# Regrouping sixteen batch tiles into chunks of 2, 3, 4, 4 and 3, and moving one exponential behind a copy

## The chip, the cores and the metric

The kernel runs on one NeuronCore of a Trainium2 chip. The core has TensorE (PE in the profile), VectorE (DVE), ScalarE (ACT), GpSimd (POOL) and SyncE (SP), each with its own in-order program, and DMA queues that SP, ACT and POOL feed. The metric is the device time of one execution in microseconds; lower is better.

## The reference, cut to what matters

A recommendation model scores 2048 items (B). A history of 50 item embeddings per item is weighted by a softmax attention; the five features are gated, paired, sent through two cross layers of 1920 x 1920, and through a small head.

```python
target = item_table[item_id] + gelu(ln(item_emb @ mm_w + mm_b))
seq_emb = item_table[item_seq]                       # B x 50 x 128, gathered
x = concat([t, seq_emb, t - seq_emb, t * seq_emb])
scores = (relu(x @ aw1 + ab1) @ aw2 + ab2)[..., 0]   # masked where item_seq == 0
hist_feat = einsum('bs,bsd->bd', softmax(scores), seq_emb)
sparse = stack([like, view, item_id_feat, item_img_feat, hist_feat])
w = sigmoid(relu(mean(sparse) @ se_w1 + se_b1) @ se_w2 + se_b2)   # the gate
se = sparse * w
dnn_in = concat([se, pairwise products of se @ bil_W and se])     # B x 1920
xc = dnn_in
for i in range(2):
    xc = dnn_in * (xc @ cross_K[i] + cross_bias[i]) + xc          # 1920 x 1920 each
h = gelu(ln(xc @ w1 + b1)); h = gelu(ln(h @ w2 + b2))
out = sigmoid(h @ w3 + b3)
```

## The kernel before

The batch is 16 tiles of 128 items. A program in two kinds of parts works on them.

**The opening.** Attention, gate and pairing of the first `TILES[0]` tiles (4 before) run alone, in steps of `opening_step` on each engine. Their features stay in SBUF as X0h and X0l (a high and a low part, both fp32r). The first pass of the cross layers can't start before them.

**The chunks.** Each of the `CHUNKS` chunks (4 before, of 4 tiles each) then makes one pass over all cross weights: 30 steps (2 layers of 15 output features), each of 3 units. A unit is one weight block of 128 x 640 (320 KB), which SP fetches (L402), ACT copies to Wh (`w_hi`, L808), DVE subtracts to Wl (`w_lo`, L1148), and PE uses in 15 matmuls (`products`, L550 to L552), each of T x 128 moving columns, where T is the chunk's number of tiles. So a pass has 1350 such matmuls whatever T is, 128x128 weights each. After them `w1_products` (L581 to L583) multiplies the result by w1: 15 x T x 3 matmuls of 512 columns, while the next chunk's features come back from DRAM (`rows_load`, L814) and are split (`r_hi`, `r_lo`). The first dense layer's output of a chunk goes through the rest of the head (`fc_...` helpers) in the first ten steps of the next chunk; after the last chunk it stands alone as a tail.

**What else a step carries.** While chunk c runs, the attention of the tiles of chunk c + 1 is woven into its steps by `make_plan`. A tile has five groups of ten history rows. GROUP_STEPS says in which steps a group's transposes stand: for 4 tiles at 1 + 6j + g, for 3 tiles at 1 + 8j + g + g // 3. A group takes three steps: `grp` (transposes on PE, `copy_eT` on ACT, `times_target` on DVE), `open` (PE `hidden`, DVE `hidden_max`, L1053, PE `score`, L503) and `summed` (DVE `softmax_max`, which ends with L1067; ACT `exps` and `weigh`, L759 to L767; DVE `history`, L1087). A tile ends with `fold` (DVE), `gate` (ACT's exponential of five numbers, L772, then DVE `tail_gate_apply`, L1113), `lift` and `pair`. In steps with history, DVE waits for `weigh` before its sum.

**Gathers.** POOL issues the 800 gathers of history rows (L415) in order of tiles. The buffer `e` holds one tile's five groups, so the rows of group g of tile t are gathered once `history` has freed group g of tile t - 1 (`e_free`, L437). From tile AHEAD = TILES[0] + 1 on, POOL also waits for the landing after every five gathers (L443).

**Order.** Every engine's order is written out by hand in `step(p)`; between engines there are only semaphores. Weights are converted three units ahead (LOOK), six raw blocks are in flight (WRING). The last tile of the opening (LAST = TILES[0] - 1) splits its fifth group in two (TAPER).

The ACT part of a step before is this (L909 to L922):

```python
unit(c, 3 * k)
...
if p.n or p.layer:
    x_hi(*((c, p.layer, p.n - 1) if p.n else (c, 0, FEATS - 1)))
if p.gate is not None:
    tail_gate()
if p.grp:
    copy_eT(0)
unit(c, 3 * k + 1)
```

Of the kernel before, what the change touches and what calls it, by code (L numbers as in the profile page):

```python
# [15 lines left out]
HID = 64  # L16
FIELDS = 5
FEATS = FIELDS + FIELDS * (FIELDS - 1) // 2
TILES = (4, 4, 4, 4)
CHUNKS = len(TILES)  # L20
BASE = tuple(sum(TILES[:c]) for c in range(CHUNKS))
TPC = max(TILES)
NB = TPC * P
# [6 lines left out]
TAPER = EVEN[:NG - 1] + (((NG - 1) * GRP, 3), ((NG - 1) * GRP + 6, 2))  # L30
LAST = TILES[0] - 1
AHEAD = TILES[0] + 1

# [50 lines left out]
class Step:  # L84


    def __init__(self, chunk, k):
# [4 lines left out]
        self.fold = self.gate = self.lift = self.pair = None  # L92
        self.fc = TILES[chunk - 1] if chunk else 0

# [46 lines left out]
def build(nc, idx_d, table_d, cate_d, embT_d, rows_d, cols_d, mmw_d, aw1_d, bil_d, kx_d, w1_d, w2_d, out_d, ntiles):  # L141
    assert sum(TILES) == ntiles
    with ExitStack() as ctx:
# [96 lines left out]
        def pairs(T):  # L240
            return [range(2 * q, min(2 * q + 2, T)) for q in range((T + 1) // 2)]
# [127 lines left out]
        def fresh(c, layer, n):  # L369
            return (x1f, x0f)[layer][:, 0:TILES[c], n, :]  # L370
# [341 lines left out]
        def _(act):  # L712
            af = nc.scalar.activation

            def done(ins):
                link(act, act_done, ins)
# [11 lines left out]
            def head_fetch(t):  # L728
                b = t % SBUFS
                act.dma_start(S[:, b, 3, :], img_d[t]).then_inc(img_landed[b], DMA)  # L730


            def copy_eT(u, n=SUB):
                act.wait_ge(tp_ready, 1).then_inc(tp_ready, -1)
                act.wait_ge(eT_free, 1).then_inc(eT_free, -1)  # L735
                done(af(eT[:, u, 0:n * P], tps[:, 0:n * P], ACT.Copy))  # L736
                act.sem_inc(tp_free, 1)
                act.sem_inc(eT_ready, 1)
# [10 lines left out]
            def copy_tT(t):  # L749
                act.wait_ge(tp_ready, 1).then_inc(tp_ready, -1)  # L750
                done(af(tT[:, t % 2, :], gps, ACT.Copy))
                act.sem_inc(tp_free, 1)
                act.sem_inc(tT_ready, 1)

            def exps(t, g):
                first, n = groups(t)[g]
                act.wait_ge(sc_ready, 1).then_inc(sc_ready, -1)
                if g:
                    af(corr[:, g:g + 1], nmax[:, g - 1:g], ACT.Exp, scale=-1.0, bias=nmax[:, g:g + 1])  # L759
                done(af(pw[:, g % 2, 0:2 * n], sc[:, first:first + 2 * n], ACT.Exp, bias=nmax[:, g:g + 1], accum_out=gsum[:, g:g + 1]))  # L760
                act.sem_inc(p_ready, 1)

            def weigh(t, g):
                first, n = groups(t)[g]
                for s in range(2 * n):
                    x = e[:, first + s, :]
                    last = af(x, x, ACT.Copy, scale=pw[:, g % 2, s:s + 1])  # L767
                last.then_inc(weighed, 1)

            def tail_gate():  # L770
                act.wait_ge(gate_ready, 1).then_inc(gate_ready, -1)
                af(g5[:], g5[:], ACT.Exp, scale=-1.0).then_inc(gexp_ready, 1)  # L772

            def tail_copy(t, opened=False):
                if 0 < t <= TILES[0]:
                    act.wait_ge(dn_free, 1).then_inc(dn_free, -1)
                elif t:
                    act.wait_ge(dnn_stored, DMA * (t - TILES[0]))
                if opened:
                    act.wait_ge(tp2_ready, 1).then_inc(tp2_ready, -1)  # L780
                    done(af(dn[:, 0:FIELDS, :].rearrange("p s b -> p (s b)"), tps2, ACT.Copy))
                    act.sem_inc(tp2_free, 1)
                else:
                    act.wait_ge(tp_ready, 1).then_inc(tp_ready, -1)
                    done(af(dn[:, 0:FIELDS, :].rearrange("p s b -> p (s b)"), tps, ACT.Copy))
                    act.sem_inc(tp_free, 1)
                act.sem_inc(S_free, 1)
                act.sem_inc(seT_ready, 1)

            def tail_store(t):  # L790
                act.wait_ge(dn_full, 1).then_inc(dn_full, -1)
                act.dma_start(dnn_d[t], dn[:, 0:FEATS, :]).then_inc(dnn_stored, DMA)
# [24 lines left out]
            def r_hi(c, k):  # L817
                for i, (a, _) in enumerate(LOADS):
                    if k == a:
                        act.wait_ge(rows_landed[i], c * DMA)  # L820
                act.wait_ge(x0_free, 1).then_inc(x0_free, -1)
                T = TILES[c]
                af(X0h[:, 0:T, k, :], x1f[:, 0:T, k, :], ACT.Copy).then_inc(hi_done, 1)

            def x_hi(c, layer, n):
                act.wait_ge(xnew_ready, 1).then_inc(xnew_ready, -1)
                Xh = X1h if layer == 0 else X0h
                af(Xh[:, 0:TILES[c], n, :], fresh(c, layer, n), ACT.Copy).then_inc(xhi_done, 1)
# [6 lines left out]
            def fc_gelu1(j, bank=FCB):  # L835
                act.wait_ge(fT_ready, 1).then_inc(fT_ready, -1)
                for k in range(H1 // P):
                    last = af(h1_T(j)[:, k, :], xps[:, bank, k * P:(k + 1) * P], ACT.Gelu, scale=col("g1", k), bias=col("lb1", k))
                done(last)
                if bank == FCB:  # L840
                    act.sem_inc(bank4_free, 1)
                act.sem_inc(g_ready, 1)

            def fc_gelu2(js, bank=FCB):
                act.wait_ge(fT_ready, 1).then_inc(fT_ready, -1)
                n = len(js)
                for k in range(H2 // P):
                    last = af(g2T(js, k), xps[:, bank, n * k * P:n * (k + 1) * P].rearrange("p (t b) -> p t b", t=n),
                              ACT.Gelu, scale=col("g2", k), bias=col("lb2", k))
                done(last)  # L850
                if bank == FCB:
                    act.sem_inc(bank4_free, 1)
                act.sem_inc(g_ready, 1)

            def fc_exp(c):
                T = TILES[c]
                act.wait_ge(logits_ready, 1).then_inc(logits_ready, -1)
                if c:
                    act.wait_ge(out_stored, c * DMA)
                done(af(probs[0:T, :], mps[0:T, 0:P], ACT.Exp, scale=-1.0, bias=neg_b3[0:T, :]))  # L860
                act.sem_inc(bank4_free, 1)
                act.sem_inc(lexp_ready, 1)

            def fc_out(c):
                act.wait_ge(probs_ready, 1).then_inc(probs_ready, -1)
                act.dma_start(out_d[BASE[c]:BASE[c] + TILES[c], :], probs[0:TILES[c], :]).then_inc(out_stored, DMA)
# [5 lines left out]
            def unit(c, b):  # L872

                if c * STREAM + b + LOOK < TOTAL:
                    w_hi(c * STREAM + b + LOOK)
# [22 lines left out]
            def step(p):  # L898
                c, k, T = p.chunk, p.k, p.fc

                if c and k == 0:
                    r_hi(c, FEATS - 1)
                if T and k == T + 6:
                    fc_exp(c - 1)
                if T and k == T + 7:
                    fc_out(c - 1)
                if p.pair is not None:
                    tail_copy(p.pair)
                unit(c, 3 * k)  # L909
                if p.fetch is not None:  # L910
                    head_fetch(p.fetch)
                if p.summed:
                    exps(*p.summed)
                    weigh(*p.summed)
                if p.n or p.layer:
                    x_hi(*((c, p.layer, p.n - 1) if p.n else (c, 0, FEATS - 1)))
                if p.gate is not None:
                    tail_gate()

                if p.grp:  # L920
                    copy_eT(0)
                unit(c, 3 * k + 1)  # L922
                if T and 2 <= k < T + 2:
                    fc_gelu1(k - 2)

                if p.grp:
                    copy_eT(1)
                elif p.swing is not None:
                    copy_tT(p.swing)
                if T and k == T + 3:  # L930
                    fc_gelu2(pairs(T)[0])
                if T > 2 and k == T + 4:
                    fc_gelu2(pairs(T)[1])
                unit(c, 3 * k + 2)
                if p.pair is not None:
                    tail_store(p.pair)
                if T and k in (1, T + 2):
                    fc_sd(T)
# [23 lines left out]
            for c in range(CHUNKS):  # L962
                for p in chunks[c]:
                    step(p)
                w1_stage(c)
# [478 lines left out]
```

## Time and profile before

| what | value |
|---|---|
| time, median of 2 runs | 2119.64 us (2118.11 to 2121.18) |
| span of the profiled execution | 2115.6 us |
| PE busy | 1937.3 us, 92% |
| DVE busy | 1337.0 us, 63% |
| ACT busy | 904.3 us, 43% |
| POOL busy | 894.1 us, 42% |
| DMA | 220.31 MB, mean 104 GB/s |

How to read it: a record's duration of a matmul is modelled and overlaps the next one's, so a rate is read from the distance between two starts. "Idle before" in brackets is how long the engine had nothing to do ahead of the row, and what released it (DVEq, ACTq, POOLq, PEq: the engine's own sequencer at a semaphore wait of that line). PEclk is the clock that TensorE was granted, 1.00 being 2.4 GHz and 0.50 being 1.2 GHz. Rows of a window give, after the window's length, each engine's busy microseconds.

### The profile page before, as it was taken

To read this page: it belongs to the slowest core of one execution; us is meant where nothing else is said; L and a number is where in the kernel's file an instruction comes from. 1 tells how busy PE (TensorE), PEld (TensorE's weight loads), DVE (VectorE), ACT (ScalarE), POOL (GpSimd) and SP (SyncE) were. 2 spreads that over 40 slices of the span, in tenths; PEclk is the share of its full clock that TensorE was granted. 3 is DMA by queue.
4 is the path that set the end of the run, shared out by engine and by line. 5 is a ranking of instruction groups with operands and counts; after the bars stand their busy time and mean duration, and the time that the engine had idled before them with its cause. 6 is when DMAs were issued, how large, how long until landed. Compare 5 with 4: busy or idle time off the path is not lost. (4 is left out here: it accounts for less than half of the span.)

```text
span 2115.6 us, 32889 instructions
## 1 busy us (share of the span) xinstructions
PE 1937.3 (92%) x9608; PEld 1518.8 (72%) x9608; DVE 1337.0 (63%) x2242; ACT 904.3 (43%) x1969; POOL 894.1 (42%) x854
## 2 busy tenths in 40 slices
PE   1765659999999999999999999999999999999997
PEld 1444437777777887777777886777777888888885
DVE  4564564767777755667777755666777664445543
ACT  1443443444444335654445235654445243322223
POOL 7777776555655512555555601555560000000000
PEclk7666568999999999999999999999999999999998
DMA  5111123334434452334434452334432442333330
GB/s 164 50 51 50 49 51 102 104 102 129 120 109 122 143 190 68 100 95 127 118 111 123 148 175 63 100 111 115 120 107 90 129 158 81 89 99 96 97 91 15
DMA packets 99679, 220.31 MB, mean 104 GB/s; under 512 B 21792, under 2 KB 27184, under 8 KB 99376
## 3 DMA queue, kind: packets, MB, share of 16 engines
q1 hardware_dynamic: 63072, 136.90, 21.5%
q0 software_dynamic: 27136, 55.63, 10.4%
q10 hardware_dynamic: 9296, 25.70, 3.2%
q8 instruction: 80, 1.31, 0.3%
q14 instruction: 95, 0.78, 0.1%
HBM read 205.29 MB, written 12.85 MB: 103 GB/s over the span
## 5 line engine op out<-in xcount | busy, mean ns | idle before, releaser
L415 POOL DMA_INDIRECT e<-in_item_table,idx_all x800 | 842.9, 1054 | 651.9 <-issue 303.8
L1148 DVE TENSOR_TENSOR Wl<-raw,Wh 128x640 fp32r<-128x640 f32 (+1 forms) x420 | 338.2, 805 | 286.6 <-DVEq L1147 283.0
L808 ACT ACTIVATE Wh<-raw 128x640 fp32r<-128x640 f32 (+1 forms) x420 | 301.8, 722 | 494.7 <-ACTq L807 493.7
L550 PE MATMUL xps<-X0h,Wh 128*128 128x512 f32 x900 | 364.7, 405 | 0.0
L550 PE MATMUL xps<-X1h,Wh 128*128 128x512 f32 x900 | 359.4, 399 | 0.0
L552 PE MATMUL xps<-X0h,Wl 128*128 128x512 f32 x900 | 352.1, 391 | 0.0
L551 PE MATMUL xps<-X0l,Wh 128*128 128x512 f32 x900 | 351.7, 391 | 0.0
L552 PE MATMUL xps<-X1h,Wl 128*128 128x512 f32 x900 | 351.0, 390 | 0.0
L551 PE MATMUL xps<-X1l,Wh 128*128 128x512 f32 x900 | 350.7, 390 | 0.0
L767 ACT ACTIVATE e<-e,pw 128x128 f32<-128x128 f32 x800 | 242.8, 388 | 15.4 <-ACTq L138 15.4
L552 PEld LDWEIGHTS xps<-X0h,Wl 128*128 128x128 f32 x900 | 169.4, 188 | 37.2
L552 PEld LDWEIGHTS xps<-X1h,Wl 128*128 128x128 f32 x900 | 168.9, 188 | 36.5
L550 PEld LDWEIGHTS xps<-X0h,Wh 128*128 128x128 f32 x900 | 169.8, 189 | 34.1 <-issue 2.1
L550 PEld LDWEIGHTS xps<-X1h,Wh 128*128 128x128 f32 x900 | 169.2, 188 | 33.6 <-issue 1.0
L551 PEld LDWEIGHTS xps<-X0l,Wh 128*128 128x128 f32 x900 | 170.1, 189 | 31.2
L551 PEld LDWEIGHTS xps<-X1l,Wh 128*128 128x128 f32 x900 | 169.4, 188 | 32.2
L1087 DVE TENSOR_REDUCE hist<-e 128x128 f32<-128x1280 f32 (+1 forms) x65 | 156.0, 2399 | 49.3 <-DVEq L1085 49.3
L736 ACT ACTIVATE eT<-aps 128x640 f32<-128x640 f32 x141 | 98.1, 696 | 166.6 <-ACTq L735 166.1
L1039 DVE TENSOR_TENSOR teT<-eT,tT 128x1280 f32<-128x1280 f32 x79 | 117.7, 1490 | 64.3 <-DVEq L1037 64.3
L492 PE MATMUL hps<-eT,A 128*64 128x512 f32 (+2 forms) x640 | 137.4, 509 | 19.7 <-PEq L486 19.6
L467 PE MATMUL aps<-ident,e 128*128 128x128 f32 x700 | 109.7, 290 | 37.9 <-issue 27.5
L496 PE MATMUL hps<-teT,A 128*64 128x512 f32 (+2 forms) x640 | 134.4, 499 | 0.0
(149 smaller groups left out, 2181.4 us busy)
## 6 DMA issues: line engine op xcount, KB each, us to landing
raw<-in_cross_K SPq DMA_DIRECT2D x360, 320.0 KB
raw<-in_w SPq DMA_DIRECT2D x60, 256.0 KB
e<-in_item_table,idx_all POOLq DMA_INDIRECT x800, 2.5
dnn_scratch<-dn ACTq DMA_DIRECT2D x12, 960.0 KB, 4.2
x1f<-dnn_scratch ACTq DMA_DIRECT2D x3, 2048.0 KB, 9.3
x1f<-dnn_scratch ACTq DMA_DIRECT2D x3, 1792.0 KB, 15.0
dn<-in_embT SPq DMA_DIRECT2D x1, 1024.0 KB, 5.3
img_scratch<-dn ACTq DMA_DIRECT2D x1, 1024.0 KB, 4.6
```

The source lines that it names most:

```text
L415: nc.gpsimd.indirect_dma_start(out=dst, out_offset=None, in_=table, in_offset=bass.IndirectOffsetOnAxis(ap=idx_all[:, t, s:s + 1], axis=0) ...
L467: last = nc.tensor.transpose(tps[:, s * P:(s + 1) * P], e_sub(t, g, u, s), ident[:])
L492: last = mm(hsum[u * HID:(u + 1) * HID, a:b], A12[:], eT[:, u, a:b], start=True, stop=False)
L496: last = mm(hsum[u * HID:(u + 1) * HID, a:b], A3[:], teT[:, u, a:b], start=False, stop=True)
L550: m0 = mm(out, wh, Xh[:, 0:T, k, :], start=(k == 0), stop=False)
L551: m1 = mm(out, wh, Xl[:, 0:T, k, :], start=False, stop=False)
L552: m2 = mm(out, wl, Xh[:, 0:T, k, :], start=False, stop=(k == FEATS - 1))
L767: last = af(x, x, ACT.Copy, scale=pw[:, g % 2, s:s + 1])
L808: af(Wh[:, split_slot(w), 0:n], raw[:, rs, 0:n], ACT.Copy).then_inc(hi_done, 1)
L1039: v.tensor_tensor(teT[:].rearrange("p u (s b) -> p (u s) b", b=P), eT[:].rearrange("p u (s b) -> p (u s) b", b=P), tT[:, par:par + 1, :].t ...
L1087: done(v.tensor_reduce(hist[:] if g else acc[:, par, :], x, AX.X, ALU.add))
L1148: v.tensor_tensor(Wl[:, rs, 0:n], raw[:, rs, 0:n], Wh[:, slot, 0:n].bitcast(F32), ALU.subtract).then_inc(lo_done, 1)
```

## The change

`TILES` becomes five chunks of 2, 3, 4, 4 and 3 tiles. The opening then prepares two tiles, and five passes over the cross weights are made instead of four. LAST becomes 1 and AHEAD 3; the largest chunk is still 4 tiles, so no buffer changes its size. And in ACT's step, the gate's exponential is issued after the first copy of transposes.

```diff
-TILES = (4, 4, 4, 4)
+TILES = (2, 3, 4, 4, 3)
...
                 if p.n or p.layer:
                     x_hi(*((c, p.layer, p.n - 1) if p.n else (c, 0, FEATS - 1)))
+                if p.grp:
+                    copy_eT(0)
                 if p.gate is not None:
                     tail_gate()
-
-                if p.grp:
-                    copy_eT(0)
                 unit(c, 3 * k + 1)
```

## Rows read from the trace of the kernel before

**Rows 1.** The profile's first part: busy time and its share of the span.
```profile
PE 1937.3 (92%) x9608; PEld 1518.8 (72%) x9608; DVE 1337.0 (63%) x2242; ACT 904.3 (43%) x1969; POOL 894.1 (42%) x854
```

**Rows 2.** Windows: opening, four chunks, tail. Columns: length, PE, PEld, DVE, ACT, POOL, PEclk, DMA.
```profile
0.00:324.40 324.40, 177.34 (x824) 121.24 (x825) 173.12 (x354) 118.90 (x325) 248.75 (x246) 0.65 0.25 69
324.40:778.40 454.00, 453.65 (x2325) 356.98 (x2325) 316.31 (x512) 202.61 (x458) 256.53 (x241) 1.00 0.43 126
778.40:1250.30 471.90, 463.91 (x2395) 365.15 (x2394) 328.63 (x545) 230.09 (x496) 223.98 (x212) 1.00 0.40 119
1250.30:1724.30 474.00, 465.36 (x2395) 365.73 (x2394) 326.72 (x538) 230.21 (x496) 164.88 (x156) 1.00 0.37 110
1724.30:2083.30 359.00, 359.00 (x1603) 296.50 (x1601) 180.92 (x268) 107.54 (x163) 0.00 (x0) 1.00 0.31 90
2083.30:2115.60 32.30, 18.04 (x74) 13.23 (x72) 11.31 (x29) 14.96 (x31) 0.00 (x0) 0.76 0.00 1
```

**Rows 3.** Timeline of PE, last chunk: first and last of 52 matmuls of 512 columns.
```profile
2000.09 0.39 PE L551 MATMUL xps<-X1l,Wh 128*128 128x512 f32 x1
...
2011.65 0.39 PE L551 MATMUL xps<-X1l,Wh 128*128 128x512 f32 x1
```

**Rows 4.** Timeline of DVE: the gates of the first and third opening tile.
```profile
122.79 0.83 DVE L1113 TENSOR_TENSOR S<-S,tiny 128x640 f32<-128x640 f32 x1
...
263.10 0.83 DVE L1113 TENSOR_TENSOR S<-S,tiny 128x640 f32<-128x640 f32 x1
```

**Rows 5.** Timeline of PE: scores (matmuls of two columns) ending two neighbouring steps.
```profile
623.53 1.17 PE L503 MATMUL hps<-cols,hidT 128*128 128x2 f32 x10
...
638.51 1.17 PE L503 MATMUL hps<-cols,hidT 128*128 128x2 f32 x10
```

**Rows 6.** Timeline of PEld: the weight loads of one of these scores.
```profile
623.31 1.31 PEld L503 LDWEIGHTS hps<-cols,hidT 128*128 128x128 f32 x10
```

**Rows 7.** Timeline of DVE, first chunk, layer 0: from one group's `softmax_max` to the next's.
```profile
396.51 0.21 DVE L1067 TENSOR_SCALAR nmax<-tiny,nmax 128x1 f32<-128x1 f32 x1
...
399.98 0.82 DVE L1053 TENSOR_TENSOR hidT<-hps,negT 128x640 f32<-128x640 f32 x1 [1.83 <-DVEq L1052]
400.72 0.21 DVE L1074 SCALAR_TENSOR_TENSOR rsum<-rsum,corr,gsum 128x1 f32<-128x1 f32 x1
401.19 2.46 DVE L1087 TENSOR_REDUCE hist<-e 128x128 f32<-128x1280 f32 x1 [0.26 <-DVEq L1085]
...
410.21 0.21 DVE L1067 TENSOR_SCALAR nmax<-tiny,nmax 128x1 f32<-128x1 f32 x1
```

**Rows 8.** Timeline of ACT: the weighing that belongs to the first of these.
```profile
397.61 3.04 ACT L767 ACTIVATE e<-e,pw 128x128 f32<-128x128 f32 x10 [0.18 <-ACTq L138]
```

**Rows 9.** Groups by line and shape (mean ns after the comma): DVE at 512 and 256 columns.
```profile
L1165 DVE TENSOR_TENSOR x0f<-X0h,X0l 128x512 f32<-128x512 f32 x60 | 41.7, 695 | 14.3 <-DVEq L1153 10.7 <-DVEq L138 2.9
...
L1218 DVE TENSOR_TENSOR dn<-xps,rows 128x256 f32<-128x256 f32 x16 | 6.7, 417 | 9.6 <-DVEq L1217 9.6
```

**Rows 10.** Timeline of DVE: the first chunk's first history sum, after which e is freed.
```profile
371.16 2.47 DVE L1087 TENSOR_REDUCE acc<-e 128x128 f32<-128x1280 f32 x1 [0.26 <-DVEq L1085]
```

**Rows 11.** Timeline of POOL: the first gather that this frees, and the 150th history row from it on.
```profile
374.61 1.01 POOL L415 DMA_INDIRECT e<-in_item_table,idx_all  x1 [11.49 <-POOLq L437]
...
658.48 0.95 POOL L415 DMA_INDIRECT e<-in_item_table,idx_all  x1 [0.30 <-issue]
```

**Rows 12.** DMA issues: size of one, median us to landing (`rows_load`, its larger part).
```profile
x1f<-dnn_scratch ACTq DMA_DIRECT2D x3, 2048.0 KB, 9.3
```

**Rows 13.** The line of the gate's exponential: its records, and ACT's waits ahead of it.
```profile
L772 ACT ACTIVATE tiny<-tiny x16: 189/194/211, 121.8 to 1649.5; 128x5 f32<-128x5 f32 x16
...
  ACTq L771: 22.1, 4
```

**Rows 14.** Timeline of PE: a wait inside the third chunk.
```profile
1315.54 0.88 PE L604 MATMUL xps<-ident,dn 128*128 128x128 f32 x3 [3.50 <-PEq L602]
```

**Rows 15.** Window around it, columns as in the windows above.
```profile
1300.00:1330.00 30.00, 26.50 (x133) 20.48 (x131) 18.54 (x31) 16.79 (x33) 14.43 (x14) 0.94 0.29 82
```

## Prediction

> **What bounds the kernel now.** I read the page's busy shares first, then a table of windows by stage, then timelines. PE is busy 92% of the span [rows 1]. By stage it is the bound in all four chunks (full in the first and the last, 98% in the others) and not in the opening: there 324.4 us pass with PE at half of its time and at a granted clock of 0.65, while POOL is busy 77% of it with gathers [rows 2]. A chunk's PE time comes out of one number: 52 matmuls of 512 columns start within 11.56 us, so one per 226.7 ns [rows 3]. A pass has 1350 of them and w1_products 180, so 1530 x 0.2267 = 346.9 us. The first chunk took 454.0 [rows 2], so the attention of four tiles costs PE 107.1, or 26.8 a tile. The two middle chunks took 18 to 20 more than the first, the head of the chunk before. The last, with the head and no tiles, took 359.0, so 12.1 for the head alone.
>
> **The opening.** It gets two tiles shorter. The gates of the first and third tile are 140.3 us apart [rows 4], that is 70.2 a tile, paced by 50 gathers; the last tile's taper keeps its distance to the first product. New opening: 324.4 - 140.3 = 184.1 us. Saved: 140.3.
>
> **What a pass costs now.** The work of the two tiles doesn't vanish: chunks must weave 14 tiles instead of 12, 2 x 26.8 = 54 us of PE. The columns that PE streams stay the same, 16 tiles' worth, but there are 1350 matmuls more, and what each costs beyond its columns is 226.7 - 512/2.4 = 13.4 ns. If that is a fixed cost, one of 256 columns takes 120 ns and one of 384 takes 173.4, and the fifth pass adds 18 us; if it scales with the columns, 113 and 170. 128x128 weight loads alone, beside matmuls of two columns, come (1.31 - 0.19)/9 = 124 ns apart [rows 6], and their matmuls (1.17 - 0.25)/9 = 102 ns [rows 5]. So a load is barely covered by 256 columns; I take 120 and keep 113 and 125 as ends. By PE alone the new chunks would be: first, 162 + 20 (w1) + 80 (3 tiles) = 263 us; second, 234 + 31 + 107 + 9 (head of two tiles) = 381; and the sum of all would be 2047. A rule of the Trainium skill ("TensorE: Matmul & The Clock Gate", Back-to-back issue gap) gives columns/2.4 + 2.5 ns, so 109 for 256 and 216 for 512, where the trace has 226.7; by it the first chunk's PE time would be 15 us less than with 120. None of this decides, because the first two chunks won't be PE's.
>
> **First chunk: VectorE.** The weights' conversion is the same per pass whether it serves two tiles or four, and so is a group's work. DVE was busy 316.3 us in the first chunk and 180.9 in the last [rows 2]. The last has no reloaded rows to split (15 x 0.69 = 10) but has the head (about 14), so a pass without tiles is 177 and a tile costs (316.3 - 177)/4 = 34.8. At 256 columns an operation takes 417 ns against 695 at 512 [rows 9]; 135 of a pass's operations have the chunk's width (3 and 5 in the steps of the two layers, 15 for the rows), so 0.27 less each, together about 36. First chunk: 177 - 36 + 3 x 34.8 = 245 us busy. Busy isn't demand: between two groups DVE takes 13.70 us, of which it waits 1.83 [rows 7]; of the other 11.87 some 1.3 are handshakes of 0.24 to 0.26, so demand is 1.14 times busy: 280. Next, DVE waits for ACT's weighing: that begins 1.1 us after the start of L1067 and takes 3.04 [rows 7, 8], so the history sum can't start before 4.2 us after L1067, and at two tiles DVE has only about 2.5 to 3 us of other work in between. That is 1.3 us for each of 15 groups: 20. Last, in steps without a full set of group work (the first, the last five, and two of each tile's eight) PE is longer by 1 to 4 us, which the three units of lead only partly even out: 18. Sum 318. Without these last two costs it would be 280. Each step of a full group takes some 12.5 us on DVE against 45 x 0.12 + 4.8 = 10.2 on PE (4.8 being what a group adds: a step is 623.53 to 638.51 [rows 5], less 10.2 of products).
>
> **The floor under the first chunk: gathers.** From tile 3 on (counted from 0; AHEAD) POOL waits after every five rows. There, from the sum that frees `e` (371.16 + 2.47 = 373.6) to the end of the 150th row (659.4) are 285.8 us [rows 10, 11], 95.3 a tile, and landing adds 1.5. Tile 3's gathers can't start before the first group of tile 2 is summed, some 33 us into the chunk; tiles 3 and 4 need 2 x 95 + 2, so tile 4 is complete at 225, and then come about 47 us of steps and 24 of w1: 296. The w1 stage is 20 us at PE's pace for 15 blocks and the rows of three tiles; rows of four took 9.3 us to land [rows 12], and here PE reaches the point where they are due after 5.4 instead of 10.9, so I put 24 to 28.
>
> **Second chunk: gathers.** It weaves four tiles at a step of 7.8 us of products instead of 10.2, but the gathers keep their pace. Freed 49.2 us after the chunk's start before (373.6 - 324.4), they are freed at about 40 now (three steps shorter by 2.4, plus the head of two tiles). 40 + 285.8 + 1.5 = 327 for the fourth tile's last group; in the first chunk before, 413 (to the start of w1) - 337 = 76 us of steps followed that point, here 6.6 steps x 2.4 less, 60; and 33 for w1: 420. DVE's demand comes close to it (177 - 17 + 139 + 7 = 306 busy, x 1.14 = 349, plus 16 of waiting), so 421. PE alone would need 381.
>
> **The rest.** Third chunk, four tiles with the head of three: 474.0 - 5 = 469. Fourth, three tiles woven: 472.5 - 26.8 = 446. Fifth, three tiles wide, nothing woven: 359.0 - 1350 x 0.0533 - 45 x 0.2267 = 277. Tail 32.3 less a tile's share, 27. The exponential: ACT waited 22.1 us ahead of it in 4 waits [rows 13], all four in the opening, whose code isn't changed; in chunks the vector engine has folded a step earlier. I cost the swap at 0: the copy comes 0.2 us sooner, and DVE needs the exponential only after `times_target`, which needs both copies anyway. If that cover were gone it would be 1.1 us for each of 14 tiles, 15 us; in the other direction it can't give back more than 0.2 x 14 = 3.
>
> **Sum.** 184.1 + 318 + 421 + 469 + 446 + 277 + 27 = 2142 us of span, against 2115.6; the profiled run lies 4.0 under the median of the runs, so 2146.
>
> **The rivals.**
> Gathers alone (near the floor): if DVE keeps up through elasticity, the first chunk is 296 and the second 416: 2142 - 27 = 2115, time 2119. For it: DVE's 280 without waits is under 296. Against it: both waits are there in the trace of before. 13%.
> Slower still, by TensorE's clock: with DVE as bound, PE gets its units 5 to 6 us apart where a history sum lies between two conversions, and idles in between. After a wait of 3.50 us in the third chunk [rows 14] the window's granted clock fell to 0.94 [rows 15], and in the opening, with such waits in every step, it was 0.65 [rows 2]. The first chunk's PE time of 263 would at 0.65 to 0.75 be 350 to 400, so 32 to 80 us more: 2178 to 2226. It decides once PE idles in most group steps; once PE is late it has no gaps, which holds the clock up, so only part of it is likely. A rule of the Trainium skill says the same, that a loop whose PE waits between bursts falls back to half rate (same page, HAM oscillation); the opening's rows agree. 22%.
> Faster: PE stays the bound, 2047 + 4 = 2051. It needs DVE demand under 8.8 us a step and gathers at 75 us a tile, and the trace shows 95. 5%.
> The swap costs: the exponential late behind a copy whose transposes are late, +15: 2161. 4%.
> My forecast, 2120 to 2175 around 2146: 56%.
>
> **How the numbers follow.** Two per cent is about what a measurement of this kernel can tell from no change; that is 2077 and 2162. Under 2077 lies only the PE-bound case: 0.05. Over 2162 lie the clock case and the upper part of the forecast (first chunk 335, second 432, a narrow matmul of 125 ns or more): 0.22 + 0.12 = 0.34. The rest, 0.61, is within. The range leaves out the PE-bound case and the upper half of the clock case: 2108 to 2192.
>
> **What would show it.** First products at about 184 us; DVE over 80% busy in the steps of the first chunk that carry groups, and PE with idle ahead of L550 there; about 318 us for that chunk, 421 for the next, with transposes (L467) waiting for gathers near its step 23; PE full again from the third chunk on. It is wrong if the 256-column matmuls start far from 120 ns apart, if the first chunk runs at a clock under 0.9, or if gathers come faster than 95 us a tile.

## The result, and the profile after

The changed kernel takes 2210.53 us (median; 2207.99 to 2213.07) against 2119.64: 1.0418 times as long, 95% interval 1.0401 to 1.0435. The profiled execution has a span of 2206.2 us, 90.6 more than before. So the change makes the kernel slower by 4%, where the prediction had 2146 us and a range of 2108 to 2192.

The first part of the profile of the kernel after, the counterpart of [rows 1], with the granted clock in 40 slices of the span:

```profile
span 2206.2 us, 37209 instructions
PE 1963.1 (89%) x10958; PEld 1653.4 (75%) x10958; DVE 1434.5 (65%) x2484; ACT 988.2 (45%) x2128; POOL 889.1 (40%) x854
PEclk6867988999999998999999999999999999999998
```

No engine looks full, and PE lost three points. The table of windows by stage says more. Here it is for the kernel after, the counterpart of [rows 2] and with its columns (length, PE, PEld, DVE, ACT, POOL, PEclk, DMA share, GB/s). The stages are: opening; steps and w1 of the first chunk; steps and w1 of the second; third chunk; fourth; steps and w1 of the fifth; tail.

```profile
0.00:183.20 183.20, 80.65 (x428) 56.01 (x429) 97.50 (x218) 63.37 (x169) 139.42 (x141) 0.70 0.29 83
183.20:510.60 327.40, 268.42 (x1946) 241.93 (x1945) 225.92 (x408) 149.62 (x348) 195.05 (x186) 0.89 0.47 136
510.60:543.40 32.80, 22.92 (x92) 15.98 (x91) 21.32 (x38) 16.91 (x33) 0.00 (x0) 1.00 0.65 227
543.40:939.90 396.50, 360.21 (x2178) 319.60 (x2179) 279.27 (x492) 195.13 (x447) 202.85 (x197) 0.97 0.40 117
939.90:979.70 39.80, 33.45 (x138) 26.08 (x136) 23.99 (x38) 18.70 (x33) 17.32 (x15) 0.96 0.73 240
979.70:1448.80 469.10, 464.06 (x2376) 364.35 (x2377) 325.17 (x537) 225.94 (x490) 225.94 (x212) 0.99 0.40 119
1448.80:1895.20 446.40, 440.17 (x2197) 349.10 (x2197) 290.34 (x471) 201.90 (x418) 108.48 (x103) 1.00 0.35 104
1895.20:2147.30 252.10, 248.35 (x1424) 245.19 (x1423) 148.36 (x244) 93.85 (x148) 0.00 (x0) 0.99 0.40 118
2147.30:2177.70 30.40, 30.40 (x135) 25.04 (x134) 13.29 (x22) 9.48 (x15) 0.00 (x0) 1.00 0.32 90
2177.70:2206.20 28.50, 14.47 (x56) 10.12 (x54) 9.30 (x24) 13.25 (x27) 0.00 (x0) 0.76 0.00 0
```

| stage | predicted | measured | miss |
|---|---|---|---|
| opening | 184.1 | 183.2 | -0.9 |
| first chunk (2 tiles wide, weaves 3) | 318 | 360.2 | +42.2 |
| second chunk (3 wide, weaves 4) | 421 | 436.3 | +15.3 |
| third chunk (4 wide, weaves 4) | 469 | 469.1 | 0 |
| fourth chunk (4 wide, weaves 3) | 446 | 446.4 | 0 |
| fifth chunk (3 wide, weaves none) | 277 | 282.5 | +5.5 |
| tail | 27 | 28.5 | +1.5 |

The opening gave its 141 us. The chunks took back 1994.5 - 1758.9 = 235.6 us, where 172 were forecast. Two thirds of the miss stand in the first chunk. There PE is busy 268 of 327 us, and DVE only 226, 69%: neither is full, so the stage must be read by its waits. DVE's in the first chunk's steps, longest first, in the kernel after (total, times, longest one), and then the longer ones of ACT and of PE:

```profile
DVE Wl L1147 <- DVEq L1146: 33.5, 35, 3.0
DVE hist L1086 <- DVEq L1084: 15.5, 12, 2.3
DVE hidT L1052 <- DVEq L1051: 7.2, 15, 0.8
ACT Wh L808 <- ACTq L807: 48.3, 54, 6.6
ACT X0h L828 <- ACTq L826: 40.8, 7, 9.1
ACT corr L759 <- ACTq L757: 38.1, 12, 5.7
PE aps L467 <- PEq L465: 29.8, 9, 6.2
```

(DVE's line numbers are one lower than before: L1147 is `w_lo`, L1086 the history sum, L1052 `hidden_max`.) All three engines wait for one another. How, a stretch of 11 us shows. Timeline of DVE, kernel after, sixth step of the first chunk:

```profile
237.56 0.21 DVE L1066 TENSOR_SCALAR nmax<-tiny,nmax 128x1 f32<-128x1 f32 x1
237.70 0.82 DVE L1147 TENSOR_TENSOR Wl<-raw,Wh 128x640 fp32r<-128x640 f32 x1
238.45 0.48 DVE L1170 SCALAR_TENSOR_TENSOR x1f<-xps,cols,x1f 128x256 f32<-128x256 f32 x1
...
241.83 2.35 DVE L1086 TENSOR_REDUCE hist<-e 128x128 f32<-128x1280 f32 x1 [2.24 <-DVEq L1084]
...
245.04 0.82 DVE L1147 TENSOR_TENSOR Wl<-raw,Wh 128x640 fp32r<-128x640 f32 x1 [0.26 <-DVEq L1146]
```

And of ACT at the same time:

```profile
238.66 3.03 ACT L767 ACTIVATE e<-e,pw 128x128 f32<-128x128 f32 x10 [0.19 <-ACTq L138]
241.59 0.40 ACT L828 ACTIVATE X1h<-x1f 128x256 fp32r<-128x256 f32 x1
241.90 0.68 ACT L736 ACTIVATE eT<-aps 128x640 f32<-128x640 f32 x1
243.00 0.74 ACT L808 ACTIVATE Wh<-raw 128x640 fp32r<-128x640 f32 x1 [0.41 <-ACTq L807]
```

DVE's `softmax_max` (it ends with L1066) releases ACT's weighing (3.03 us), DVE's sum waits 2.24 us for that and then runs 2.35, and the next `w_lo` stands behind the sum. On ACT, X1h, a copy of transposes and the weights' high part stand behind the weighing. So 245.04 - 237.70 = 7.34 us pass between the starts of two conversions. PE uses up one unit in 15 x 0.12 = 1.8 us, so three units of lead are gone in 5.4.

This is what the text below calls the loop: DVE waits for ACT, ACT waits for DVE, each in its own fixed order, and neither is full.

### The profile page after: what moved, and what is told of

It is laid out like the page before. It is cut to its first block and busy times, and to the rows that moved or that the text cites. A ratio compares the mean times of both kernels' runs of the same rounds, so it can differ in the third digit from the quotient of the medians.

```text
span 2206.2 us, 37209 instructions
## 1 busy us (share of the span) xinstructions
PE 1963.1 (89%) x10958; PEld 1653.4 (75%) x10958; DVE 1434.5 (65%) x2484; ACT 988.2 (45%) x2128; POOL 889.1 (40%) x854
## 5 line engine op out<-in xcount | busy, mean ns | idle before, releaser
L1147 DVE TENSOR_TENSOR Wl<-raw,Wh 128x640 fp32r<-128x640 f32 (+1 forms) x525 | 422.7, 805 | 280.5 <-DVEq L1146 278.7
L808 ACT ACTIVATE Wh<-raw 128x640 fp32r<-128x640 f32 (+1 forms) x525 | 374.6, 720 | 458.9 <-ACTq L807 449.9
L550 PE MATMUL xps<-X1h,Wh 128*128 128x384 f32 (+2 forms) x1125 | 409.2, 364 | 18.6 <-PEq L544 14.5
L550 PE MATMUL xps<-X0h,Wh 128*128 128x384 f32 (+2 forms) x1125 | 413.1, 367 | 10.3 <-PEq L548 8.0
L552 PE MATMUL xps<-X1h,Wl 128*128 128x384 f32 (+2 forms) x1125 | 397.2, 353 | 0.0
L551 PE MATMUL xps<-X1l,Wh 128*128 128x384 f32 (+2 forms) x1125 | 397.1, 353 | 0.0
L551 PE MATMUL xps<-X0l,Wh 128*128 128x384 f32 (+2 forms) x1125 | 396.5, 352 | 0.0
L552 PE MATMUL xps<-X0h,Wl 128*128 128x384 f32 (+2 forms) x1125 | 396.2, 352 | 0.0
L551 PEld LDWEIGHTS xps<-X0l,Wh 128*128 128x128 f32 x1125 | 219.1, 195 | 15.5
L1086 DVE TENSOR_REDUCE hist<-e 128x128 f32<-128x1280 f32 (+1 forms) x65 | 155.3, 2389 | 63.9 <-DVEq L1084 63.7
L467 PEld LDWEIGHTS aps<-ident,e 128*128 128x128 f32 x750 | 89.5, 147 | 88.8 <-issue 83.7
L736 ACT ACTIVATE eT<-aps 128x640 f32<-128x640 f32 (+1 forms) x151 | 105.0, 695 | 105.2 <-ACTq L735 104.3
L1038 DVE TENSOR_TENSOR teT<-eT,tT 128x1280 f32<-128x1280 f32 x79 | 117.8, 1491 | 45.9 <-DVEq L1036 45.1
L492 PE MATMUL hps<-eT,A 128*64 128x512 f32 (+2 forms) x640 | 125.3, 470 | 14.9 <-PEq L486 14.3
## 6 DMA issues: line engine op xcount, KB each, us to landing
x1f<-dnn_scratch ACTq DMA_DIRECT2D x2, 2048.0 KB, 10.7
x1f<-dnn_scratch ACTq DMA_DIRECT2D x2, 1344.0 KB, 12.2
```

The lines of the kernel that those rows point to most:

```text
L467: last = nc.tensor.transpose(tps[:, s * P:(s + 1) * P], e_sub(t, g, u, s), ident[:])
L492: last = mm(hsum[u * HID:(u + 1) * HID, a:b], A12[:], eT[:, u, a:b], start=True, stop=False)
L550: m0 = mm(out, wh, Xh[:, 0:T, k, :], start=(k == 0), stop=False)
L551: m1 = mm(out, wh, Xl[:, 0:T, k, :], start=False, stop=False)
L552: m2 = mm(out, wl, Xh[:, 0:T, k, :], start=False, stop=(k == FEATS - 1))
L808: af(Wh[:, split_slot(w), 0:n], raw[:, rs, 0:n], ACT.Copy).then_inc(hi_done, 1)
```

## Experiments

All ratios are to the kernel before, with a 95% interval; the kernel after stands at 1.0418. The kernel before was run again beside each group of experiments, with medians of 2120.6 to 2122.1 us, so times of different groups compare within some 2 us. Where a change of a stage is given, it is between the two profiled executions, against the same stage of the kernel after.

### Which half of the change

**Chunks alone**: the kernel before with the new `TILES`.

```diff
-TILES = (4, 4, 4, 4)
+TILES = (2, 3, 4, 4, 3)
```

> The five chunks with the gate's exponential left where it was before. Theory (the swap is worth nothing, all of the loss is the chunks'): the time of the changed kernel, 2210 us, within 5 us. Rival (the swap makes the copy of transposes hold up the gate, about 1 us for each of 14 tiles woven into chunks): 2195 us, since the swap's cost is gone.

Measured: 2210.78 us, 1.0427 [1.0410, 1.0444]. **Swap alone**: the kernel after with the old `TILES`.

```diff
-TILES = (2, 3, 4, 4, 3)
+TILES = (4, 4, 4, 4)
```

> Four chunks of four tiles as before, with the exponential behind the first copy. Theory: 2120 us within 3 us, since the exponential never waited in the chunks of the kernel before (idle 0.0 in all twelve). Rival (the swap costs about 1 us a tile): 2132 us; a gain could be at most some 3 us.

Measured: 2119.86 us, 0.9996 [0.9986, 1.0006]. The swap is worth nothing either way, as costed; all of the loss is the regrouping's. The first of these kernels also shows how well a stage repeats, since it differs from the kernel after by the swap alone: 327.1 us for 327.4 in the first chunk's steps, 393.6 for 396.5 in the second's.

### What the gathers' waits cost

`AHEAD = 16` takes away POOL's wait after every five gathers. In its place stands the opening's wait, one a group, for the landing of the group before. In the kernel after:

```diff
-AHEAD = TILES[0] + 1
+AHEAD = 16
```

> The changed kernel, with gathers issued in all tiles as in the opening, without a wait for the landing after every five (AHEAD = 16). The trace of the changed kernel has 95 us a tile with these waits, and 69 to 73 without them in the opening. Theory G (gathers bind the second chunk's first 23 steps, the loop between vector and scalar engine binds the first chunk): steps of the first chunk stay at 327 us within 4, those of the second fall from 396 to about 375 to 385, total near 2195. Theory L (the loop binds both chunks, the gathers only just keep up): second chunk within 5 us of 396, total 2205 to 2211.

Measured: 2201.68 us, 1.0383 [1.0360, 1.0406]. The steps of the first chunk stay (327.2), those of the second fall from 396.5 to 388.3; the later stages stay within half a microsecond. The same edit in the kernel before:

> The kernel before (four chunks of four), with the waits for landing after every five gathers taken out. Control for the same edit in the changed kernel, where it took 8 us from the second chunk. Theory (PE binds every chunk of four tiles): within 3 us of 2120. Rival (the gathers hold up the last tile's groups there too): 5 to 15 us less.

Measured: 2120.53 us, 0.9998 [0.9988, 1.0007]: there PE hid the gathers wholly. So the gathers hold the second chunk, but by 8 us only, where this run was expected to bring 11 to 21. Something else stands right below them.

### Is it TensorE, or its clock

The first rival of weight in the prediction was a falling clock, and the clock did fall: 0.89 in the first chunk's steps. This kernel leaves out a third of the products of the first two chunks (low part of the features times the high part of the weights; one matmul stays, because it signals).

```diff
+                    if c > 1 or (c and layer == 0 and n == 0 and kg == 0 and i == 0):
-                    m1 = mm(out, wh, Xl[:, 0:T, k, :], start=False, stop=False)
+                        m1 = mm(out, wh, Xl[:, 0:T, k, :], start=False, stop=False)
```

> The changed kernel with a third of the products (those with the low part of X) left out in its first two chunks, so that part of the result is missing: PE has 54 us less in the first and 78 us less in the second. Theory V: PE and its clock don't set these chunks; the first chunk's steps fall by under 12 us, the second's by under 25. Rival C (PE is what is late, because its clock is halved in part of the first chunk): the first falls by 35 us or more, the second by 50 or more, total under 2130.

Measured: 2211.12 us, 1.0416 [1.0394, 1.0438]. Windows of this kernel, steps of the first and the second chunk (columns as above):

```profile
184.20:509.80 325.60, 229.04 (x1497) 198.72 (x1496) 225.44 (x408) 149.54 (x350) 195.83 (x187) 0.82 0.47 137
542.30:943.20 400.90, 312.59 (x1730) 265.63 (x1731) 277.90 (x490) 194.59 (x447) 208.24 (x197) 0.87 0.39 115
```

Some 450 matmuls less in each stage (54 us at 120 ns, 78 at 173), PE busy 39 and 48 us less, the clock lower still (0.82 and 0.87), and the stages hardly move: 325.6 for 327.4, 400.9 for 396.5. PE's products do not bind the first two chunks. With less for PE to do its waits grew and the clock fell further, and no cost of that is seen. This takes away the 22% rival's mechanism, though its time (2178 to 2226) holds the result.

The transfer of the weights is one more candidate, and no run tests it. The trace speaks against it in the first chunk's steps: the DMA share is 0.47 at 136 GB/s there, and the w1 stages move up to 240 GB/s. An estimate from the bytes on the weights' queue in this trace has every block landed 0.2 us or more (median 3.3) before ACT takes it up.

### Is it the order on ACT

DVE's longest wait is for the high part of the weights (33.5 us). Here ACT makes the step's second high part first, ahead of the features' high part, the copy of transposes and the exponential.

```diff
+                unit(c, 3 * k + 1)
                 if p.n or p.layer:
                     x_hi(*((c, p.layer, p.n - 1) if p.n else (c, 0, FEATS - 1)))
                 if p.grp:
                     copy_eT(0)
                 if p.gate is not None:
                     tail_gate()
-                unit(c, 3 * k + 1)
```

> The changed kernel, with the scalar engine's conversion of the step's second weight block issued ahead of x_hi, the first copy and the exponential, not behind them. In the changed kernel the vector engine waits 33.5 us in the first chunk's steps and 31.0 in the second's for this conversion (ahead of L1147), 1.4 to 3 us a step, because the conversion stands behind x_hi, which itself waits for the vector engine. Theory L (this loop sets the step): first chunk's steps from 327 to about 300 to 310, second's down by up to 15, total 2170 to 2190. Rival V (the vector engine's own work sets the step, the wait only moves elsewhere): both chunks within 6 us, total 2204 to 2212. If the copies become late behind the second block, it gets slower than 2211.

Measured: 2199.70 us, 1.0375 [1.0358, 1.0392]; first chunk's steps 323.8, second's 391.0. The theory that this one wait sets the pace wanted 300 to 310 for the first chunk and falls. The other theory (the wait only moves) allowed 6 us a chunk, which both keep; its total of 2204 or more was not kept. DVE's waits in the first chunk's steps of this kernel:

```profile
DVE teT L1038 <- DVEq L1036: 17.5, 11, 2.6
DVE hist L1086 <- DVEq L1084: 15.2, 12, 2.2
DVE Wl L1147 <- DVEq L1146: 15.0, 33, 3.0
```

The wait ahead of `w_lo` fell from 33.5 to 15.0, and ahead of `times_target` (L1038) it rose from 1.7 to 17.5, since the copies of transposes now stand later on ACT. The wait moved. Only where no group is woven did it go: in the last five steps of the chunk DVE waits 2.6 us ahead of `w_lo` instead of 6.8, and they take 43.0 us instead of 47.4. The 24 steps of the woven tiles gained nothing.

Together with `AHEAD = 16`:

> The changed kernel with both orders tried alone before: the second weight block converted ahead of x_hi, and gathers without the waits after every five. Alone they took 11 and 9 us. If the two chunks are bound at different places they add: 2188 to 2194 us, still over the 2120 of the kernel before. If they are not additive: 2199.

Measured: 2197.32 us, 1.0368 [1.0350, 1.0386], span 2188.6. The first chunk's steps are 324.0, the second's 386.0. The two edits don't add up. Alone they took 10.8 and 8.9 us off the median and 13.9 and 8.3 off the span; together 13.2 off the median and 17.6 off the span. On top of the first, the second brings 2.4 us by medians, which these intervals don't tell from nothing. This is the fastest kernel of the study that computes everything in five chunks, and it is still 3.7% slower than the kernel before.

### Taking work out of the chain of DVE and ACT

Three kernels leave out a part of the work between two conversions, each another part, with order and waits as they are.

Half of the history sum (of the woven tiles, 5 of a group's 10 rows are summed on DVE):

```diff
-                x = e[:, first:first + 2 * n, :].rearrange("p s d -> p d s")
+                x = e[:, first:first + (n if t >= TILES[0] else 2 * n), :].rearrange("p s d -> p d s")
```

> The changed kernel, where the history sum of the tiles woven into chunks reads five of a group's ten rows, so half of the sum is left out: about 1.2 us less vector time a group, no wait changed. Theory V (the vector engine's own work sets the steps of the narrow chunks): 15 groups, so the first chunk's steps fall from 327 by 14 to 20 us; the second's from 396 by 8 to 20 (20 groups, but the gathers stop it sooner); the chunks of four tiles stay; total 2175 to 2190. Rival P (waits for other engines set them): under 6 us in all.

Half of the weighing (of the woven tiles, ACT weighs 5 of 10 rows):

```diff
-                for s in range(2 * n):
+                for s in range(n if t >= TILES[0] else 2 * n):
                     x = e[:, first + s, :]
```

> The changed kernel where the scalar engine weighs five of a group's ten rows in the tiles woven into chunks (the others go into the sum unweighed): 1.5 us less scalar time a group, the vector engine's work is unchanged. It measures the wait for the weighing that the prediction put at 20 us for the first chunk; the trace has 15.5 us ahead of L1086 there. Theory V: the first chunk's steps fall by 12 to 18 from 327, the second's by 0 to 6 (gathers), total 2190 to 2200. Rival (another wait takes its place, as with the weights' order): under 5 us in the first chunk.

A shorter low part of the weights (in the first two chunks DVE makes 384 of its 640 columns, and the products of the other two blocks take the high part instead):

```diff
+                if LOOK <= w < 2 * STREAM and w % STREAM < BLOCKS:
+                    n = 3 * P
...
+                    wl = wl if c > 1 or i < 3 else wh
                     m0 = mm(out, wh, Xh[:, 0:T, k, :], start=(k == 0), stop=False)
```

> The changed kernel where, in the first two chunks, the low part of a weight block is made for three of its five 128-column pieces (384 columns, not 640) and the products use the high part for the other two: part of the precision is left out. PE's work, the scalar engine's and the transfers are unchanged; the vector engine's part of a pass that doesn't shrink with the chunk's width falls by about 0.27 us a block, 24 us in 90 blocks. Theory V: the first chunk's steps fall by 18 to 26 from 327, the second's by 3 to 12 (gathers stop it), total 2175 to 2190. Rival (waits set the steps, not work): under 8 us in the first chunk.

| kernel | time | ratio | first chunk's steps | second's |
|---|---|---|---|---|
| after | 2210.53 | 1.0418 | 327.4 | 396.5 |
| half history sum (DVE) | 2192.9 | 1.0348 [1.0325, 1.0371] | 310.5 | 400.2 |
| half weighing (ACT) | 2190.4 | 1.0323 [1.0305, 1.0340] | 316.0 | 395.7 |
| short low part (DVE) | 2189.8 | 1.0335 [1.0312, 1.0358] | 314.0 | 389.8 |

The first chunk's steps of these three, in that order:

```profile
183.50:494.00 310.50, 259.87 (x1947) 234.17 (x1946) 208.97 (x408) 149.25 (x348) 190.85 (x182) 0.92 0.49 142
```
```profile
186.50:502.50 316.00, 264.38 (x1946) 238.45 (x1945) 226.17 (x408) 129.96 (x276) 186.19 (x183) 0.92 0.48 140
```
```profile
185.00:499.00 314.00, 264.70 (x1946) 240.11 (x1946) 202.70 (x409) 150.90 (x351) 187.35 (x185) 0.90 0.49 141
```

The first takes 17.0 us of DVE's time and the stage loses 16.9. The second takes nothing from DVE (226.17 against 225.92) and 19.7 from ACT, of which 11.4 come off; DVE's wait ahead of its sum fell by about as much, from 15.5 to 4.4. The third takes 23.2 from DVE, 13.4 come off; here DVE's waits for ACT and PE grew (ahead of `w_lo` from 33.5 to 37.0, ahead of `hidden_max` from 7.2 to 10.5). So the first chunk is bound neither by DVE's volume nor by ACT's, but by the loop that goes through both: work taken from either part shortens the stage, by 0.6 to 1.0 of what is taken, and reordering it or lightening PE hardly does.

Not all of the expectations were met. In the first chunk the half sum's was (14 to 20); the half weighing fell just short of its 12 to 18, and the short low part well short of its 18 to 26. In the second chunk the half sum was to bring 8 to 20 and brought nothing.

The second chunk hardly answers to the half sum (+3.7) or the half weighing (-0.8), and only a little to the short low part (-6.7). Its steps can be split at the gathers: to the end of the sum that frees `e`, then the 150 gathers of three tiles with 1.5 us for the landing, then the rest up to w1.

| kernel | to the first freeing | 150 gathers | rest | steps |
|---|---|---|---|---|
| after | 45.9 | 284.0 | 66.6 | 396.5 |
| half history sum | 46.0 | 288.3 | 65.9 | 400.2 |
| half weighing | 44.3 | 284.9 | 66.5 | 395.7 |
| short low part | 44.3 | 282.0 | 63.5 | 389.8 |

The gathers keep their 282 to 288 us whatever is taken from DVE or ACT; the short low part gains more before and behind them than in them. If gathers hold the chunk and the loop stands just below, taking both away must bring more than the sum of each alone. The half sum with `AHEAD = 16`:

> The changed kernel with both half of the history sum left out (five of ten rows are summed in the tiles woven into chunks) and the gathers without their waits. Alone, the first left the second chunk's steps at 400 us, the second took them from 396 to 388. Theory B (there two bounds lie within 10 us of each other, the vector engine's work and the gathers): with both gone the second chunk's steps fall to 365 to 378, total 2168 to 2182. Rival (a third thing holds that chunk): 385 or more, total 2185 or more.

Measured: 2165.12 us, 1.0211 [1.0194, 1.0228]. Windows of the second chunk's steps, first with the gathers free alone, then with both edits:

```profile
543.40:931.70 388.30, 355.12 (x2179) 314.11 (x2180) 279.84 (x492) 194.34 (x447) 222.74 (x212) 0.98 0.42 123
```
```profile
531.00:903.10 372.10, 350.53 (x2178) 310.89 (x2179) 257.17 (x492) 194.94 (x447) 223.14 (x212) 0.99 0.44 128
```

Gathers free alone -8.2, half the sum alone +3.7, both -24.4, within the 365 to 378 us that were expected (the total, 2168 to 2182, was undershot by 3). So two bounds lie within 10 us of each other in the second chunk, and the lower one is the loop of DVE and ACT.

### What a narrow pass costs by itself

The chunks as 4, 4, 4, 2 and 2: the last pass is two tiles wide and weaves nothing.

```diff
-TILES = (2, 3, 4, 4, 3)
+TILES = (4, 4, 4, 2, 2)
```

> Chunks of 4, 4, 4, 2 and 2: the opening is that of the kernel before, and the last chunk of four is cut in two, so the price of a fifth pass stands alone. By PE alone the chunks would be 454, 472, 420, 248, 188 and the total about 2135 us. Theory V: the narrow chunk that weaves two tiles and a head takes 280 to 310, not 248, and the last, narrow and without tiles, 200 to 225, not 188, since a step there needs 4 to 5 us of vector work plus a round trip to the scalar engine against 5.4 of PE; total 2190 to 2215.

Measured: 2258.33 us, 1.0639 [1.0621, 1.0657]; more than either expectation. Its third to fifth chunk take 978.6 us, where the third and fourth of the kernel before took 833.0: this fifth pass costs 146 us by itself, the opening being as before. The steps of its fourth chunk (2 tiles wide, weaving 2, with the head of four) and of its fifth:

```profile
1674.40:1982.90 308.50, 249.54 (x1820) 226.89 (x1819) 200.35 (x367) 144.81 (x304) 54.15 (x50) 0.91 0.38 113
2013.90:2208.90 195.00, 176.60 (x1386) 172.38 (x1387) 124.00 (x224) 80.15 (x135) 0.00 (x0) 0.97 0.52 150
```

With its w1 the fourth took 339.5 us, where 280 to 310 were expected; the fifth with its w1 fell within its 200 to 225. In the fifth, 30 steps would take 30 x 5.4 = 162 us at PE's pace. It took 195.0, though no attention is woven and DVE is busy 64% of it. Some of that is the head's steps at its start. But the last four steps in layer 0 take 5.4 us, as PE needs, and the last ten in layer 1 take 6.5 to 6.8. The loop shows in the last steps of the first chunk of the kernel after too. DVE, first chunk, layer 1:

```profile
485.23 0.43 DVE L1179 TENSOR_TENSOR x0f<-x0f,X1l 128x256 f32<-128x256 f32 x1
487.11 0.82 DVE L1147 TENSOR_TENSOR Wl<-raw,Wh 128x640 fp32r<-128x640 f32 x1 [1.46 <-DVEq L1146]
...
493.61 0.83 DVE L1147 TENSOR_TENSOR Wl<-raw,Wh 128x640 fp32r<-128x640 f32 x1 [1.46 <-DVEq L1146]
```

The two `w_lo` that wait stand 493.61 - 487.11 = 6.50 us apart. Between L1179's end and the next `w_lo`, ACT makes the features' high part (485.93, 0.42 us) and only then the next weights' high part: DVE waits 1.46 us because the two stand in that order. The kernel that turns this order round took 4.4 us off these last five steps, as said above.

## Why the prediction was wrong

**Right: opening, matmuls, gathers, the wide chunks.** First products at 183.2 (184.1 forecast). Matmuls start 120 ns apart at 256 columns, 173 to 174 at 384 and 227 at 512, so the fixed part is about 13.4 ns as in [rows 3]: the value taken, not its ends. The Trainium skill ("TensorE: Matmul & The Clock Gate", Back-to-back issue gap) gives columns/2.4 + 2.5 ns for a single matmul in isolation, by it 109 ns. The trace decides for 120. In the second chunk the 150 waited gathers took from 589.3 to 871.8 and 1.5 more, 284.0 us (287 forecast from [rows 10, 11]). Third and fourth chunk came within 0.4 us, so the price of a woven tile on PE (26.8) and of a head (12.1) hold where PE is the bound. The swap cost nothing.

**Right in kind: DVE in the first chunk, gathers in the second, PE from the third on.** DVE's busy time in the first chunk was 225.9 + 21.3 = 247.2 us, forecast 245. But "DVE over 80% busy in the steps that carry groups" was wrong: it was 70% in the 24 steps of the woven tiles (188.9 of 268.8 us).

**The step that failed** is the one from DVE's busy time to the length of the first chunk: 245 x 1.14 = 280, plus 20 for one wait on ACT, plus 18 for steps in which PE was to be longer, 318. In its steps DVE stood idle 101.5 us. The wait that was priced came out near its price (15.5 ahead of the history sum, for 20). The longest one, 33.5 us ahead of `w_lo`, had no term, though the first chunk's steps of the kernel before have 30.6 us of it, hidden behind a full PE there. And the 18 us were given to PE, which a third of its products left out shows not to bind. What stood in its place is the loop: 360.2 us. Its parts:

- *The last five steps*: 47.4 us, taken as 27 (PE's 5.4 each). They carry no group, so they were given to PE; but a step of layer 1 costs 6.5 by the loop above even when nothing else stands in it (the last ten steps of the chunks 4, 4, 4, 2 and 2), and here the gate and pairing of the last woven tile and the first work on the next one do (13.2 and 10.5 in the longest two). 20 us.
- *The woven tiles*: 84.5 + 96.6 + 87.7 = 268.8 us for 24 steps, some 260 by the prediction's working. The longest step of each tile takes 15 to 16.5 us, the shortest 6.1 to 8.7, and the three units of lead, 5.4 us of PE, do not even that out. 9 us.
- *The first step*: 11.2 us, taken as 5.4. ACT and PE serve the target's transpose between two weights (a wait of 2.89 us ahead of `w_lo` at 194.12). The same step took 13.1 us before, where PE alone needs 10.2, so it could be read there. 6 us.
- *w1*: 32.8, taken as 26. The larger part of the reloaded rows landed 7.5 us after its issue, sooner than the 9.3 of [rows 12], which were for four tiles; but high and low parts of rows and weights then alternate between ACT and DVE with waits, at 65% DVE busy. 7 us.

**Second chunk, 436.3 for 421.** Three terms were too small. The first freeing came 45.9 us after the chunk's start, not 40. The prediction's own working gives more than 40: 49.2 less three times 2.4 is 42, and the head comes on top; the third step took 14.8 us, where it was 14.9 before, and 11.1 us of the fourth passed until the freeing, where it was 9.8. From the last landing to w1 were 66.6 us, not 60, because the last three steps (10.0, 10.2, 9.6) had shrunk by 0.6 to 1.0 us and not by 2.4. w1 took 39.8 for 33, of which PE stood 4.1 us at its start, waiting for an output bank that DVE frees only with the chunk's last feature (945.57, released at L574; the reloaded rows were not yet asked for then). The prediction's line for DVE failed here as in the first chunk: it gave 349 + 16 = 365 us, which it called close to 420. With the gathers free the chunk takes 388.3 + 40.1 = 428.4, and the half sum on top shows that the loop sets it. So 421 came near by the gathers' term, while the second bound was put 63 us too low.

**Fifth chunk and tail, 7 us together.** The fifth chunk's miss is in the four steps with the head: 13.9, 10.7, 10.8 and 10.7 us, where 12.2, 12.6, 12.6 and 12.6 less 2.4 each were forecast. The first of them alone is 4.1 us over. Scaling every step by its columns was wrong there; why that step got longer is not tested.

**The rivals.** "Gathers alone" and "PE stays the bound" fell. The rival by the clock had the right size by luck: it named 2178 to 2226 from a cause that wasn't there. The clock did fall, to 0.89 in the first chunk's steps, which the prediction had also named as a sign of being wrong; but with a third of the products gone the stage stayed as long. By the Trainium skill the clock falls in a loop whose PE waits between bursts ("TensorE: Matmul & The Clock Gate", HAM oscillation). The trace agrees: 0.89, and 0.82 where PE waited more. The price of a bound by DVE and ACT together was missing from the rivals and from the range: the forecast's upper end for the first chunk was 335, and it took 360.

**What stays open.** That work taken from DVE's or ACT's part of the loop shortens the stage is shown; which order of the two engines' programs would be best isn't. The one reordering that was tried brought 0.4%. The extra of the w1 stages, of the first step and of the fifth chunk was read from the trace alone, not tested, and so was the room that the weights' transfers had.

## What to carry to other kernels

When a pass gets narrower, its fixed work (weight conversions, small vector operations, one group of attention) stays, and the bound can pass from an engine with much slack around it to a loop through two in-order engines that are only 69% and 46% busy. Price such a stage by walking one period of the loop (who waits for whom, what stands behind the waiting instruction), not by busy time times a factor; and look at stages of the kernel before in which the same steps already ran longer than the bound's pace. A shorter opening bought with one more pass over the weights pays only if the pass is cheap at its new bound: here 141 us were saved and 236 paid.

## What the runs showed of the hardware

- The granted clock in a stage can fall without a cost, where TensorE is not the bound: 0.82 over 325.6 us with PE busy 229, against 0.89 over 327.4 with PE busy 268.
- What a matmul with its own 128x128 weight load costs here beyond its columns is one fixed amount of about 13 ns: 120, 173 to 174 and 227 ns from start to start at 256, 384 and 512 columns. At 256 columns the load still costs nothing more, though loads beside matmuls of two columns stand 124 ns apart [rows 6].
